# Interleaving the down projection of one FFN slab with the gate projection of the next in a macaron layer on 8 cores

## The reference

```python
x = x + 0.5 * ffn(layernorm(x), w_gate, w_up, w_down)
x = x + attn(layernorm(x), Wq, Wv, Wo, Wg, beta, ln_gamma, ln_beta)
x = x + 0.5 * ffn(layernorm(x), w_gate, w_up, w_down)

def ffn(x, w_gate, w_up, w_down):            # integer weights, scaled by 1/127
    gate = einsum('bsd,hd->bsh', x, wg)
    up   = einsum('bsd,hd->bsh', x, wu)
    return einsum('bsh,dh->bsd', silu(gate) * up, wd)
```

## Time and profile before

| what | value |
|---|---|
| time, median of 2 runs | 7249.58 us (7248.32 to 7250.85) |
| profiled execution, device time | 7250.46 us |
| its span, slowest core (core 7) | 7248.9 us |
| spans of all cores | 7232.3 to 7248.9 us |
| granted TensorE clock, mean over a core's span | 0.918 to 0.920 of full |
| PE busy | 5711.2 us, 79% of the span |
| DVE busy | 2081.9 us, 29% |
| ACT busy | 1474.4 us, 20% |

### The profile page before, as it was taken

How to read it: one execution, slowest core, us unless ns; L and a number is a source line. 1 busy time by engine, 2 the same in 40 slices (tenths; PEclk the granted TensorE clock), 3 DMA queues, 4 the chain that set the end, 5 groups by cost and what they waited for, 6 DMA issues and landing times.

```text
span 7248.9 us, 81015 instructions; the slowest of 8 cores (7232.3 to 7248.9 us)
## 1 busy us (share of the span) xinstructions
PE 5711.2 (79%) x29138; PEld 2835.3 (39%) x29138; DVE 2081.9 (29%) x3929; ACT 1474.4 (20%) x2342; POOL 173.1 (2%) x112
## 2 busy tenths in 40 slices
PE   0012998685998799786998799786999699786899
PEld 0011444443443344443443344443444344443444
DVE  0012124244123213344123213344123213444123
ACT  1000212222211211322211221322211221322211
POOL 0000000000000000000000000000000000000000
PEclk9999999787999899887999899887999799887999
DMA  8733013200013000100013110100012110100001
GB/s 98 118 97 94 24 47 81 71 1 24 28 43 98 31 35 24 47 1 24 24 47 87 38 39 24 47 1 24 24 41 78 45 47 24 47 1 24 24 35 70
DMA packets 152525, 322.11 MB, mean 44 GB/s; under 512 B 112336, under 2 KB 112336, under 8 KB 140048
## 3 DMA queue, kind: packets, MB, share of 16 engines
q1 hardware_dynamic: 134016, 239.10, 10.1%
q0 software_dynamic: 18128, 77.84, 6.1%
HBM read 291.74 MB, written 88.08 MB: 52 GB/s over the span
## 4 chain that ended last, share of the span: by engine, by line
PE 70%; DVE 9%; DMA 7%; issue 5%; ACT 4%; another core or an unknown queue 3%; DVEq 1%; SPq 0%; ACTq 0%; POOL 0%; POOLq 0%
PE PSB L608 18%; PE PSB L635 18%; PE PSB L660 15%; PE PSB L718 9%; PE PSB L846 5%; PE PSB7b L570 2%; ACT XN L576 2%; DMA TSTB<-nat_g 2%; DVE STATS L541 1%; DMA TSTB<-nat_u 1%; DVE ACC L674 1%; ACT ACC L839 1%; PE PSB7b L835 1%; ACT TMPTM L783 1%
## 5 line engine op out<-in xcount | busy, mean ns | idle before, releaser
L645 DVE TENSOR_TENSOR H<-SG,PSB 128x512 bf16<-128x512 bf16 x768 | 527.7, 687 | 2622.4 <-PE PSB L635 2622.4
L660 PE MATMUL PSB<-WA,H 128*128 128x512 bf16 x4096 | 900.0, 383 | 25.7 <-DVE ACC L674 25.7
L625 ACT ACTIVATE SG<-PSB 128x512 bf16<-128x512 f32 x768 | 458.5, 597 | 2202.4 <-PE PSB L608 2202.4
L608 PE MATMUL PSB<-XN,WA 128*128 128x512 bf16 x4096 | 903.5, 383 | 0.6 <-ACT SG L625 0.6
L635 PE MATMUL PSB<-XN,WB 128*128 128x512 bf16 x4096 | 889.3, 379 | 0.0
L660 PEld LDWEIGHTS PSB<-WA,H 128*128 128x128 bf16 x4096 | 403.2, 99 | 519.9 <-issue 45.2
L608 PEld LDWEIGHTS PSB<-XN,WA 128*128 128x128 bf16 x4096 | 403.8, 99 | 493.2 <-issue 19.6
L635 PEld LDWEIGHTS PSB<-XN,WB 128*128 128x128 bf16 x4096 | 401.1, 98 | 483.0
L570 PE MATMUL PSB7b<-IDN,TMPTM 128*128 128x128 bf16 x1536 | 194.0, 305 | 479.6 <-ACT XN L576 268.2
L674 DVE SCALAR_TENSOR_TENSOR ACC<-PSB,ACC 128x512 bf16<-128x512 f32 x512 | 352.0, 689 | 358.1 <-PE PSB L660 355.7
L545 ACT ACTIVATE TMPTM<-X 128x1024 bf16<-128x1024 bf16 x192 | 202.9, 1057 | 1202.6 <-DMA X<-x 505.9
(11 more groups left out here) (95 smaller groups left out, 4019.3 us busy)
## 6 DMA issues: line engine op xcount, KB each, us to landing
WA<-scr_g SPq DMA_DIRECT2D x16, 2048.0 KB, 7.6
WB<-scr_u SPq DMA_DIRECT2D x16, 2048.0 KB, 7.6
WA<-scr_d SPq DMA_DIRECT2D x16, 2048.0 KB, 7.7
o<-X POOLq DMA_DIRECT2D x16, 2048.0 KB, 7.3
X<-x POOLq DMA_DIRECT2D x16, 1024.0 KB, 9.7
WB<-scr_g SPq DMA_DIRECT2D x8, 2048.0 KB, 7.4
WA<-scr_u SPq DMA_DIRECT2D x8, 2048.0 KB, 7.4
WB<-scr_d SPq DMA_DIRECT2D x8, 2048.0 KB, 7.3
```

Source lines behind the costliest of these rows:

```text
L608: t.matmul(PSB[bank][:], wg_sl[:, SLAB * k + 128 * m:SLAB * k + 128 * (m + 1)], XN[:, S * k + 512 * g:S * k + 512 * (g + 1)], start=(k == ...
L625: s.activation(dst, PSB[bank][:], AF.Silu, scale=np32(1.0 / 127.0)),
L645: v.tensor_tensor(dst, src0, PSB[bank][:], ALU.mult),
L660: t.matmul(PSB[bank][:], H[:, S * hc + 128 * c:S * hc + 128 * (c + 1)], wd_sl[:, D * hc + 512 * n:D * hc + 512 * (n + 1)], start=(hc == 0) ...
```

## The change

The slab loop is rewritten so that the down projection of a slab is not emitted at the end of its slab. Its 32 groups are kept as a list `pending` and are emitted in the next slab, mixed with the 16 groups of gate half 0: two down groups, one gate group, two down groups, one gate group, and so on, until both lists are used up. Only then the load of the up weights is emitted, and up half 0, gate half 1 and up half 1 follow as before. Slab 0 has no pending list, and its gate half 0 is emitted as before. The down projection of the last slab is emitted alone after the loop, with its X updates, statistics and transfers. The groups, their operands, banks, slots and readers are the same as before; the debugging branches (`tap`), which are off, are removed.

The core of the diff (the bodies of the emitters are those of the old loops):

```diff
-        for j in range(nsl):
-            ...
-            if not (skip_gw0 and j == 0):
-                em.dma("wl", ... out=a[:] ..., in_=scr_g[:, j]), ..., writes=[wg_k])
-                em.dma("wl", ... out=a[:] ..., in_=scr_u[:, j]), ..., writes=[wu_k])
-            for hs in range(2):
-                (16 gate groups, then 16 up groups)
-            em.dma("wl", ... out=a[:] ..., in_=scr_d[:, j]), ..., writes=[wd_k])
-            (32 down groups)
+        pending = None
+        for j in range(nsl):
+            li = 3 * j
+            wg_sl, wg_k = slots[li % 2]
+            wu_sl, wu_k = slots[(li + 1) % 2]
+            wd_sl, wd_k = slots[(li + 2) % 2]
+            if not (skip_gw0 and j == 0):
+                em.dma("wl", lambda sy, a=wg_sl, j=j: sy.dma_start(
+                    out=a[:].rearrange("p (k h) -> p k h", h=SLAB), in_=scr_g[:, j]),
+                    reads=[f"scrT_wgate_r{r}" for r in range(HID // 128)], writes=[wg_k])
+            gates0 = gate_emitters(j, 0, wg_sl, wg_k)
+            if pending is not None:
+                gi, di = 0, 0
+                while gi < len(gates0) or di < len(pending):
+                    if di < len(pending):
+                        pending[di]()
+                        di += 1
+                    if di < len(pending):
+                        pending[di]()
+                        di += 1
+                    if gi < len(gates0):
+                        gates0[gi]()
+                        gi += 1
+                pending = None
+            else:
+                for e in gates0:
+                    e()
+            if not (skip_gw0 and j == 0):
+                em.dma("wl", lambda sy, a=wu_sl, j=j: sy.dma_start(
+                    out=a[:].rearrange("p (k h) -> p k h", h=SLAB), in_=scr_u[:, j]),
+                    reads=[f"scrT_wup_r{r}" for r in range(HID // 128)], writes=[wu_k])
+            up_block(j, 0, wu_sl, wu_k)
+            for e in gate_emitters(j, 1, wg_sl, wg_k):
+                e()
+            up_block(j, 1, wu_sl, wu_k)
+            em.dma("wl", lambda sy, a=wd_sl, j=j: sy.dma_start(
+                out=a[:].rearrange("p (k h) -> p k h", h=D), in_=scr_d[:, j]),
+                reads=[f"scrT_wdown_s{j}r{r}" for r in range(D // 128)], writes=[wd_k])
+            pending = down_emitters(j, wd_sl, wd_k, last=(j == nsl - 1))
+        for e in pending:
+            e()
```

More of the change, by code:

```diff
@@ L581, in ffn_phase, with gate_emitters, emit @@
         layer_norm_to_xn(prestats=prestats)
-        if tap:
-            em.dma("st", lambda g: g.dma_start(out=dbg_xn, in_=XN[:]),
-                   reads=[k for row in kXN for k in row], writes=["DBGXN"])
         nsl = NSLAB if DBG_SLABS is None else DBG_SLABS
-        for j in range(nsl):
[L587 to L591, removed]
-            if not (skip_gw0 and j == 0):
[L593 to L601, removed]
-            for hs in range(2):
[L603 to L606, removed]
+        slots = [(WA, "WSLOTA"), (WB, "WSLOTB")]
+        def gate_emitters(j, hs, wg_sl, wg_k):
+            ems = []
+            for g in range(4):
+                for m4 in range(4):
+                    m = 4 * hs + m4
+                    bank = (g * 4 + m4) % 2
+                    def emit(g=g, m4=m4, m=m, bank=bank, wg_sl=wg_sl, wg_k=wg_k):
                         items = [(lambda t, k=k, m=m, g=g, wg_sl=wg_sl, bank=bank:
@@ L614, in ffn_phase @@
                         em.group("tensor", items, writes=[kPSB[bank]])
[L615 to L622, removed]
@@ L623, in ffn_phase @@
                         dst = SG[:, S * m4 + 512 * g:S * m4 + 512 * (g + 1)]
-                        em.op("scalar", lambda s, dst=dst, bank=bank:
-                              s.activation(dst, PSB[bank][:], AF.Silu,
-                                           scale=np32(1.0 / 127.0)),
+                        em.op("scalar", lambda sc, dst=dst, bank=bank:
+                              sc.activation(dst, PSB[bank][:], AF.Silu,
+                                            scale=np32(1.0 / 127.0)),
@@ L627, in ffn_phase @@
                               reads=[kPSB[bank]], writes=[kSG[m4][g]],
                               war=["WGT"] + PREP_SG_KEYS)
[L629 to L655, removed]
+                    ems.append(emit)
@@ new lines, in gate_emitters, with up_block @@
+            return ems
+        def up_block(j, hs, wu_sl, wu_k):
+            for g in range(4):
+                for m4 in range(4):
+                    m = 4 * hs + m4
+                    hc = m
+                    bank = 2 + (g * 4 + m4) % 2
+                    items = [(lambda t, k=k, m=m, g=g, wu_sl=wu_sl, bank=bank:
+                              t.matmul(PSB[bank][:],
+                                       wu_sl[:, SLAB * k + 128 * m:SLAB * k + 128 * (m + 1)],
+                                       XN[:, S * k + 512 * g:S * k + 512 * (g + 1)],
+                                       start=(k == 0), stop=(k == KC - 1)),
+                              [wu_k] + [kXN[k][4 * g + i] for i in range(4)])
+                             for k in range(KC)]
+                    em.group("tensor", items, writes=[kPSB[bank]])
+                    dst = H[:, S * hc + 512 * g:S * hc + 512 * (g + 1)]
+                    src0 = SG[:, S * m4 + 512 * g:S * m4 + 512 * (g + 1)]
+                    em.op("vector", lambda v, dst=dst, src0=src0, bank=bank:
+                          v.tensor_tensor(dst, src0, PSB[bank][:], ALU.mult),
+                          reads=[kSG[m4][g], kPSB[bank]], writes=[kH[hc][g]],
+                          war=B_H)
@@ L656, in ffn_phase, with down_emitters @@
+        def down_emitters(j, wd_sl, wd_k, last):
+            ems = []
             for c in range(NCH):
@@ L658, in ffn_phase @@
                     bank = 4 + (c * 2 + n) % 3
[L659 to L686, removed]
+                    def emit(c=c, n=n, bank=bank, wd_sl=wd_sl, wd_k=wd_k, last=last):
+                        items = [(lambda t, hc=hc, c=c, n=n, wd_sl=wd_sl, bank=bank:
+                                  t.matmul(PSB[bank][:],
+                                           H[:, S * hc + 128 * c:S * hc + 128 * (c + 1)],
+                                           wd_sl[:, D * hc + 512 * n:D * hc + 512 * (n + 1)],
+                                           start=(hc == 0), stop=(hc == 7)),
+                                  [wd_k, kH[hc][c // 4]])
+                                 for hc in range(8)]
+                        em.group("tensor", items, writes=[kPSB[bank]])
+                        dst = ACC[:, D * c + 512 * n:D * c + 512 * (n + 1)]
+                        if j == 0:
+                            em.op("scalar", lambda sc, dst=dst, bank=bank:
+                                  sc.activation(dst, PSB[bank][:], AF.Copy, scale=SFIN),
+                                  reads=[kPSB[bank]], writes=[kACC[c][n]], war=WAR_ACC_A)
+                        else:
+                            em.op("vector", lambda v, dst=dst, bank=bank:
+                                  v.scalar_tensor_tensor(dst, PSB[bank][:], SFIN, dst,
+                                                         ALU.mult, ALU.add),
+                                  reads=[kPSB[bank], kACC[c][n]], writes=[kACC[c][n]])
+                        if last and n == 1:
+                            xc = X[:, D * c:D * (c + 1)]
+                            ac = ACC[:, D * c:D * (c + 1)]
+                            em.op("vector", lambda v, xc=xc, ac=ac: v.tensor_tensor(
+                                xc, xc, ac, ALU.add),
+                                reads=[kX[c], kACC[c][0], kACC[c][1]], writes=[kX[c]])
+                            if next_stats:
+                                ln_stats(c)
+                            if tail_cb is not None:
+                                tail_cb(c)
```

## The result

| | before | after |
|---|---|---|
| undisturbed executions, device time | 7248.3 to 7251.7 us | 7483.2 to 7490.9 us |
| ratio of these | 1 | 1.0328, 95% interval 1.0305 to 1.0351 |
| median over all executions of the comparison | 7661.0 us (10) | 8083.4 us (11) |
| mean over the 8 cores' spans in the profiled execution | 7241.9 us | 7476.2 us |
| mean granted clock | 0.918 to 0.920 | 0.910 to 0.911 |

In more than half of the executions of either kernel the cores of one die or of both ran at a lower granted clock, and these stand in the medians but not in the ratio, which goes by the others (called undisturbed). The change makes the kernel 3.3% slower; by the ratio that is 7487 us against the 7504 us predicted.

The account below looks back on a forecast made before the run. The prediction took the FFN as bound by matmul count at full clock. Core 0, slowest: 7241.7 + 203.5 (stalls) + 58.2 (clock) = 7503.4 us; device time 1.6 us above, median 0.9 us under, gives 7504 us; range 7411 to 7539.

Parts of the forecast that it names:

- no gain from the mixed order: In the FFN: looser banks could give back at most 26 us; the forecast took nothing as a gain.
- two stalls in each of 16 passages: PE waits for gate and up loads: 4.35 and 6.17 us on core 7, 5.55 and 7.17 us on core 0.
- the mixed read-outs: ACT and DVE read-outs in a round of two down groups and one gate group: hidden under PE's 5.18 us, cost nothing.
- Rival 3: At the passages: the loads stay hidden, not slower, time within 2% of before; chance 0.06.
- rival 1: At the stalls: PE is back before its clock comes down, 7411 to 7446 us; chance 0.12.
- rival 2: Slab loads: transfers get slower, by 1.1 us each, 7539 us, or 7559 with more clock loss; chance 0.08.
- The clock: After each of 32 stalls in the FFN passages: PE's clock comes down, 1.82 us lost each, 58.2 us in all.
- the place in the attention: PE stops 3.59 us, does 8 small matmuls, stops 1.37 us; the next 16 matmuls lose 1.82 us.
- the median of the runs is 0.9 us under the profiled execution: Last step of the sum, from the profiled execution to the median of runs: 7505.0 us becomes 7504 us.

## Where the prediction was right, and where it was wrong

**Right: what the change uncovers.** The forecast of a clearly slower kernel, with no gain from the mixed order, two stalls in each of 16 passages and nothing for the mixed read-outs, is what the waits and the runs with five leading or trailing groups show. The sum was 7504 us; the ratio gives 7487 us, inside the range of 7411 to 7539. Rival 3 (loads hidden) is out by 32 waits in the trace, rival 1 (the clock holds) by the windows, rival 2 (slower transfers) by the landings, whose medians after are 7.3 to 7.6 us on every core.

**Wrong: that the order could win only 26 us in the FFN.** The prediction called the 25.7 and 0.6 us of the earlier trace rows all that an edit of the order can win there. It left out the waits at the head of each phase, where PE waits for the layer norm: the version that mixes the transposes with the gate groups won about 175 us. For the change as made this did not matter, since it leaves the head as it was.

**The stalls: right on core 7, wrong on core 0.** Computed for core 7 were 4.35 and 6.17 us, 168.3 us in all. Its trace after has 162.3 us. For core 0 the forecast was 203.5 us, from landings of 8.6 and 8.5 us. Core 0 after, gate loads and then up loads:

```profile
DMA to landing us min/median/max: 7.2/7.5/14.2
```

```profile
DMA to landing us min/median/max: 7.2/7.4/10.6
```

Its waits are 163.6 us, 40 us under the forecast. Forecast as the slowest core with 7503.4 us, it has the shortest span of all, 7464.6 us. The slow landings of core 0 belonged to the one execution that was shown: in the kernel with the mixed round undone, which loads as before, the median of the loads into WB on core 0 is 7.5 us too. What slowed them in the first execution is open. Core 4 had 7.6 us there, but medians of 7.8 to 8.4 us by kind of load again in the first profile of the version with mixed transposes, so slow landings of a core can come back.

**The clock: right mechanism, too small a term.** Forecast were 1.82 us a stall, 58.2 us in all, after the place in the attention. Over the 8 cores the mean span grew by 7476.2 - 7241.9 = 234.3 us, of which the waits are 163.3 us in the mean. The remaining 71 us are 2.2 us a stall, and they are gone in the run with filled stalls. Directly: a window of 8 us behind a stall at a granted clock c has lost 8 x (1 - c) us of full-clock work. The first two of core 3:

```profile
861.71:869.71 8.00, 8.00 (x26) 0.68 0.00 0
949.55:957.55 8.00, 8.00 (x32) 0.84 0.00 0
```

All 32 add up to 67.4 us on core 3, 1.3 to 3.0 us each, 2.1 in the mean. The row of the attention was too low a guide probably since part of the slow time there passes in idle time and in 8 small matmuls, before the 16 whose duration I compared. After a stall in the FFN, the slow time falls on dense matmuls from the first on.

**Two errors that cancel.** That 7504 lies 17 us from 7487 is in part luck. On the slowest core I had 40 us too much for waits and 9 to 22 us too little for the clock (67 to 81 us by the windows and by the remainder on core 3). With 7.4 us landings on all cores and 2.2 us a stall, the same sum gives 7248.9 + 168.3 + 70.4 + 0.7 = 7488 us, against 7487.

**The step that failed: from a clean execution to the median of all.** The range was for executions like the two shown, 7248 and 7251 us. The median over all executions in the comparison is 8083.4 us and far outside it, and so is that of before, 7661.0, far from the 7249.6 us that I started from. The step that fails is "the median of the runs is 0.9 us under the profiled execution": it took two close times as the whole spread and gave the spread between executions no term. The runs show that this term is larger than the effect of the change: 7661.0 - 7249.6 = 411 us in the median of before, 8083.4 - 7487 = 596 us in that of after. It is not shown to come from the change: in the comparisons of the later runs the kernel before alone had medians of 7253.8, 7449.6, 7529.0 and 7802.7 us. What decides the spread stays open. No step on the change itself puts the time outside the range.

**The Trainium skill, weighed again.** In the Trainium skill, "DMA: Bandwidth & Descriptors" (Anatomy of one DMA) gives a fit from which 6.8 us follow for 2 MB, an estimate. The traces show 7.4 and 7.5 us at the median on core 7 before and 7.3 to 7.6 us after, so the rows were the better term. The Trainium skill, "TensorE: Matmul & The Clock Gate" (HAM oscillation), says that a wait for a DMA in each step takes the clock down each time. All 32 windows of core 3 agree, at 0.63 to 0.84, and the run with shorter stalls shows it for 26 of 32 stalls of about 2.4 us, and not for the other 6.

## What to carry to other kernels

When the order of groups is changed, measure for each buffer how much work stands between its last reader and the first reader of its next contents; here both loads needed 7.8 us of it and were left with 3.45 and 1.73 us. In this kernel, mixing two dense loops gained nothing where PE was already dense, and was free only while each load kept its cover; it paid where PE stood still for other engines, and not where the engine that it waited for, DVE, got more work in the same round. Do not take two close times for the spread of a kernel. A PE stall of a few us costs more than its length: here 4.2 to 5.9 us of waiting cost another 2.2 us at 1.2 GHz.

## What the runs showed of the hardware

- Filling a stall with useless matmuls made the program faster: 688 more matmuls, 148 us of them, and a mean span of 7409.4 us in place of 7476.2, with a granted clock of 1.00 on all 8 cores through the whole first FFN phase (745 to 1200 us).
- The granted clock came down behind 26 of 32 stalls of about 2.4 us, a stall of 2.26 us among them, and held through one of 2.78 us. Which it does is not settled by the length of the stall alone.
- The same 2 MB load lands after 7.4 us (core 7) or after 8.5 us (core 0) at the median, in one execution of the same program.
